# A graph network's last layer: the experts' loop by three chunks instead of four, its ends written out, and the node rows summed tile by tile

## The chip, the cores and the metric

The kernel runs on one core of a Trainium2 chip. The metric is the device time of one execution in microseconds (us), the lower the better. The engines are TensorE (PE, with its weight loads listed apart as PEld), VectorE (DVE), ScalarE (ACT), GpSimd (POOL) and SyncE (SP), which here only issues transfers.

## The reference

Four residual layers over a graph with 3125 nodes of 256 features and 50000 edges, each closed by a layernorm. The change concerns the last layer: a graph convolution, then a mixture of 64 experts, two for each node, then a batch norm over all nodes:

```python
x = gc + (feats @ W_res + b_res)
vals, idx = jax.lax.top_k(x @ Wg + bg, 2)
gates = softmax(vals)
# for each expert e: rows of the nodes that picked it
h1 = gelu(rows @ w1[e] + b1[e])          # 256 -> 512
h2 = h1 @ w2[e] + b2[e]                  # 512 -> 256
core = zeros.at[tok].add(gate * h2)
y = x + core
y = (y - mean(y, 0)) * rsqrt(var(y, 0) + 1e-5) * gamma + beta
```

All weights are float32. The 6250 picked rows fall on the 64 experts very unevenly, from 10 to 409 rows each on the inputs used. Cut into chunks of at most 128 rows of one expert each they make 81 chunks.

## The kernel before

Nodes are held in T = 25 tiles of 128 rows. The last layer ("l3") goes over these tiles: PE adds up the neighbours' rows, DVE makes the tile's rows x (`l3_x4`, L1749, into V; POOL copies them to X4), picks the two experts and gives each row a slot (`l3_top`, `l3_slots`), and POOL scatters the rows to their slots in device memory (`expert_rows_in`). Then the five engines run the functions `sync_moe`, `pe_moe`, `act_moe`, `dve_moe` and `pool_moe`, each in its own order, tied by semaphores.

The experts' loop goes over chunks c. `RING` = 4 is at once the number of chunks written out in one turn of the loop and the number of buffers for a chunk's loads: its rows `xin` (128 KB), `w1s` and `w2s` (512 KB each), the bias `b2s` (128 KB, one row spread over the partitions) and its result `yout`. The transposed rows xTs, the hidden values hTs and their three places in PSUM have two buffers each. The turns are the number of chunks over RING, rounded up.

- PE, for each c: `turn(c+2)` transposes the rows of the chunk two ahead (L554), `hidden(c+1)` makes 512 hidden columns from w1 (L562), `rows_out(c)` multiplies them by w2 (L572). Its queue is in order, so what `turn` waits for (`rows_in`) holds up all that follows.
- ACT: `gelu` (L619). DVE: copies the transposed rows (L659), scales the bias (L683), evicts the result times the gate into yout (L688, which counts `chunk_made` up), and adds yout to the running sum V2 (L694). POOL scatters yout to device memory (L760).
- SP, for each c, in this order, with n = c mod RING:

```python
ex = expert_of(c + RING)
e.wait_ge(S("chunk_turned"), c + 1)
load_rows(c + RING, n)                  # L473
e.wait_ge(S("hidden_summed"), c + 1)
load_w1(ex, n)                          # L476
e.wait_ge(S("chunk_made"), c + 3)       # counted up by 2 beforehand: chunk c is evicted
load_w2(ex, n)                          # L480
load_b2(ex, n)                          # L484
```

SP too is in order: the rows of chunk c+1+RING are issued after the w2 and the bias of chunk c+RING, and so after the eviction of chunk c.

Ahead of the loop DVE copies two chunks' transposed rows, then adds up the node rows X4 over all tiles into R2 (L667, L668), clears V2, and takes the picks and gates that PE has transposed (L582, L671, L672). The loop runs past its end: PE and ACT do a hidden stage for one chunk too many and PE two transposes too many, and SP loads RING chunks that nobody uses. After the loop V2 += R2 (L698), PE sums that over the partitions (L597), DVE subtracts the mean (L703), SP waits for the spare loads (L517) and for the stored rows (L521) and loads the experts' rows back (L526), and DVE, ACT and PE finish the batch norm and the layernorm.

Of the kernel before, what the change touches and what calls it, by code (L numbers as in the profile page):

```python
# [24 lines left out]
P = 128  # L25
# [7 lines left out]
RING = 4  # L33
# [19 lines left out]
def gnn_program(nc, A, out):  # L53
# [33 lines left out]
    NCH = MAXCH + RING  # L87

# [12 lines left out]
    with ExitStack() as ctx:  # L101
# [78 lines left out]
        nturn = sb("nturn", [1, 1], I32)  # L180
# [118 lines left out]
        for base, lot, room in ((mw, ((w1s, (KF, H), RING), (w2s, (HT, F), RING)), T * PARTS * F * 2),  # L299
                                (mx, ((yout, (F,), RING), (b2s, (F,), RING), (xTs, (F,), 2), (hTs, (HT, P), 2),  # L300
                                      (xin, (F,), RING)), 10240)):
# [11 lines left out]
        at = 2 * F * (2 * RING + 2) + 2 * 2 * HT * P  # L313
# [23 lines left out]
        pdec, px4 = psum[:, 5, P:2 * P], psum[:, 5, 0:F]  # L337

# [63 lines left out]
        def past(ph, name):  # L402
            return T * SIGNALS[name].index(ph)
# [63 lines left out]

        def sync_moe(e):
# [53 lines left out]
            e.wait_ge(S("gelu_made"), RING * turns + 1)  # L522
# [18 lines left out]
        def pe_moe(e):  # L541
# [9 lines left out]
            def turn(c, j, n, par):  # L551
                e.wait_ge(S(f"rows_in{n}"), 16 * j + 16)
                for k in range(KF):
                    mm = e.transpose(psum[:, par, k * P:(k + 1) * P], xin[n][:, k * P:(k + 1) * P], identF[:, :])  # L554
                mm.then_inc(S("chunk_turned"), 1)

            def hidden(c, j, n, par):
                e.wait_ge(S("chunk_copied"), c + 1)
                e.wait_ge(S(f"w1_in{n}"), 16 * j + 16)
                for h in range(HT):  # L560
                    for k in range(KF):
                        mm = e.matmul(psum[:, 2 + par, h * P:(h + 1) * P], w1s[n][:, k, h * P:(h + 1) * P],  # L562
                                      xTs[par][:, k * P:(k + 1) * P], start=(k == 0), stop=(k == KF - 1))
                mm.then_inc(S("hidden_summed"), 1)

            def rows_out(c, j, n, par):
                e.wait_ge(S("gelu_made"), c + 1)
                e.wait_ge(S(f"w2_in{n}"), 16 * j + 16)

                e.wait_ge(S("chunk_made"), c + 1)  # L570
                for h in range(HT):
                    mm = e.matmul(psum[:, 4 + par, 0:F], hTs[par][:, h, :], w2s[n][:, h, :],  # L572
                                  start=(h == 0), stop=(h == HT - 1))
                mm.then_inc(S("chunk_summed"), 1)

            turns = e.value_load(nturn[0:1, 0:1], min_val=1, max_val=MAXCH // RING)
# [30 lines left out]
        def act_moe(e):  # L607
# [7 lines left out]
            def gelu(c, par):  # L615
                ex = e.value_load(etab[0:1, bass.ds(c, 1)], min_val=0, max_val=NE - 1)
                e.wait_ge(S("hidden_summed"), c + 1)
                for h in range(HT):
                    mm = e.activation(hTs[par][:, h, :], psum[:, 2 + par, h * P:(h + 1) * P], ACT.Gelu,  # L619
                                      bias=b1T[:, h, bass.ds(ex, 1)])  # L620
                mm.then_inc(S("gelu_made"), 1)

            turns = e.value_load(nturn[0:1, 0:1], min_val=1, max_val=MAXCH // RING)
            gelu(0, 0)
            with e.Fori(0, turns) as j:
                for n in range(RING):
                    c, par = RING * j + n, n % 2

                    e.wait_ge(S("chunk_summed"), c)
                    gelu(c + 1, 1 - par)  # L630
# [14 lines left out]
        def dve_moe(e, st):  # L645
# [3 lines left out]
            st.done(e.tensor_scalar(eint[0:1, 0:1], pages[0:1, 0:1], float(RING - 1), None, ALU.add))  # L649
            st.done(e.tensor_scalar(nturn[0:1, 0:1], eint[0:1, 0:1], RING.bit_length() - 1, None,  # L650
                                    ALU.arith_shift_right))

# [4 lines left out]
            def copy_turned(c, par):  # L657
                e.wait_ge(S("chunk_turned"), c + 1)
                e.tensor_copy(xTs[par], psum[:, par, 0:F]).then_inc(S("chunk_copied"), 1)  # L659

            e.sem_inc(S("chunk_made"), 2)
            copy_turned(0, 0)
            copy_turned(1, 1)


            e.wait_ge(S("tile_x4_kept"), past("l3", "x4_kept") + T)
# [3 lines left out]
            e.wait_ge(S("ids_turned"), 1)  # L670
            e.tensor_copy(pick_of, psum[:, 6, 0:NCH]).then_inc(S("picks_known"), 1)  # L671
            st.done(e.tensor_copy(gate_of, psum[:, 6, NCH:2 * NCH]))  # L672
            turns = e.value_load(nturn[0:1, 0:1], min_val=1, max_val=MAXCH // RING)
            with e.Fori(0, turns) as j:
                for n in range(RING):
                    c, par = RING * j + n, n % 2

                    e.wait_ge(S("hidden_summed"), c + 1)
                    copy_turned(c + 2, par)
# [6 lines left out]
                    e.wait_ge(S(f"rows_stored{n}"), 16 * j)  # L686
                    carry_wait(e)
                    e.scalar_tensor_tensor(yout[n], psum[:, 4 + par, 0:F], gate_of[:, bass.ds(c, 1)], b2s[n], ALU.mult, ALU.add)\  # L688
                        .then_inc(S("chunk_made"), 1)

                    e.wait_ge(S("rows_added"), c + 1)
                    e.wait_ge(S("chunk_made"), c + 3)
# [43 lines left out]
        def pool_moe(e):  # L736
# [11 lines left out]
            turns = e.value_load(nturn[0:1, 0:1], min_val=1, max_val=MAXCH // RING)  # L748
            with e.Fori(0, turns) as j:
                for n in range(RING):  # L750
                    c, par = RING * j + n, n % 2
# [6 lines left out]
                    e.wait_ge(S("chunk_made"), c + 3)  # L758
# [610 lines left out]
        def _(e):  # L1369
# [364 lines left out]

            e.memset(rooms[:, 0, :], float(P))
# [13 lines left out]
            def l3_x4(i, par):  # L1749
# [3 lines left out]
                e.tensor_tensor(V[:, :], pD[0], bc["gc"][:, :], ALU.add).then_inc(S("tile_x4_made"), 1)  # L1753

# [240 lines left out]
```

## Time and profile before

| | us |
|---|---|
| median of 3 runs (1962.0 to 1967.8) | 1963.7 |
| the profiled execution | 1963.03 |
| its span in the trace | 1961.3 |
| PE busy | 1768.7 |
| PEld busy | 1423.0 |
| DVE busy | 949.3 |
| POOL busy | 492.8 |
| ACT busy | 486.4 |

The last layer's tiles end near 1538 us, the experts' loop lies between about 1551 and 1888 us, and the rest, to 1961.3 us, is the batch norm, the layernorm and the stores of the result. In the rows below a line of code is L and its number. An SPq row is a transfer being issued by SP. A PE duration in the timeline overlaps with its neighbours, while the chain's rows lie end to end.

### The profile page before, as it was taken

To read this page: it belongs to the slowest core of one execution; us is meant where nothing else is said; L and a number is where in the kernel's file an instruction comes from. 1 tells how busy PE (TensorE), PEld (TensorE's weight loads), DVE (VectorE), ACT (ScalarE), POOL (GpSimd) and SP (SyncE) were. 2 spreads that over 40 slices of the span, in tenths; PEclk is the share of its full clock that TensorE was granted. 3 is DMA by queue.
4 is the path that set the end of the run, shared out by engine and by line. 5 is a ranking of instruction groups with operands and counts; after the bars stand their busy time and mean duration, and the time that the engine had idled before them with its cause. 6 is when DMAs were issued, how large, how long until landed. Compare 5 with 4: busy or idle time off the path is not lost.

```text
span 1961.3 us, 34807 instructions
## 1 busy us (share of the span) xinstructions
PE 1768.7 (90%) x9576; PEld 1423.0 (73%) x9577; DVE 949.3 (48%) x2841; ACT 486.4 (25%) x1278; POOL 492.8 (25%) x905
## 2 busy tenths in 40 slices
PE   4888887699989999999999999999999599999961
PEld 2455555588878888788888878877777488888851
DVE  7876664444445511121221127766666734434456
ACT  0144444322223311122221111111212132233223
POOL 1122222311113300000000002217778733233314
PEclk7999998799999999999999999999999799999976
DMA  4189999899869888766658878887776499999992
GB/s 133 41 285 307 315 318 344 299 325 325 308 231 374 325 310 288 266 217 217 206 197 304 288 274 290 292 280 237 246 261 214 145 350 377 375 375 375 373 363 69
DMA packets 276800, 545.13 MB, mean 278 GB/s; under 512 B 18358, under 2 KB 201184, under 8 KB 272992
## 3 DMA queue, kind: packets, MB, share of 16 engines
q1 hardware_dynamic: 266720, 525.41, 78.6%
q0 software_dynamic: 8032, 17.63, 2.4%
q10 hardware_dynamic: 1952, 0.95, 0.3%
q8 instruction: 43, 0.70, 0.2%
q14 instruction: 53, 0.43, 0.1%
HBM read 415.12 MB, written 128.81 MB: 277 GB/s over the span
## 4 chain that ended last, share of the span: by engine, by line
PE 73%; DVE 11%; DMA 6%; issue 4%; DVEq 2%; SPq 1%; POOL 1%; ACT 1%; ACTq 0%; POOLq 0%
PE psum L1065 41%; PE psum L562 7%; PE psum L572 7%; PE psum L1162 4%; PE psum L957 4%; PE psum L954 3%; PE psum L976 2%; DMA blk<-counts_src_on_rows 2%; PE psum L1144 1%; PE psum L554 1%; PE psum L1173 1%; SPq L783 1%; DMA expert_weights<-expert_rows_out 1%; DMA counts_src_on_rows<-blk 1%; DMA route<-expert_rows_in 1%
## 5 line engine op out<-in xcount | busy, mean ns | idle before, releaser
L1065 PE MATMUL psum<-xsa,blk 128*128 128x512 f32 x2500 | 638.7, 403 | 11.9 <-DVE xsa L1631 9.7
L1065 PEld LDWEIGHTS psum<-xsa,blk 128*128 128x128 f32 x2500 | 456.8, 189 | 99.2 <-issue 12.6
L1065 PE MATMUL psum<-xsb,blk 128*128 128x512 f32 (+1 forms) x1875 | 407.9, 366 | 8.5 <-DMA blk<-counts_src_on_rows 5.2
L1065 PEld LDWEIGHTS psum<-xsb,blk 128*128 128x128 f32 x1875 | 316.1, 190 | 62.1 <-issue 8.6
L1904 POOL TENSOR_SCALAR ve<-mv 128x1 f32<-128x1 f32 x75 | 16.8, 224 | 763.1 <-DVE mv L1607 763.1
L1492 DVE TENSOR_SCALAR onehots<-counts_scratch 128x348 bf16<-128x348 f16 x464 | 161.6, 374 | 86.1 <-issue 45.8
L954 PE MATMUL psum<-onehots 128*128 128x349 bf16 x464 | 149.3, 322 | 38.7 <-DVE onehots L1497 38.2
L957 PE MATMUL psum<-zrow 128*128 128x512 bf16 x464 | 176.1, 389 | 0.0
L562 PE MATMUL psum<-route,expert_weights 128*128 128x128 f32 x1360 | 171.6, 281 | 4.3 <-DVE route L659 4.2
L562 PEld LDWEIGHTS psum<-route,expert_weights 128*128 128x128 f32 x1360 | 162.0, 195 | 6.1 <-DVE route L659 5.0
L572 PE MATMUL psum<-expert_weights,route 128*128 128x256 f32 x672 | 159.0, 380 | 0.0
L619 ACT ACTIVATE route<-psum,b1T 128x128 f32<-128x128 f32 x340 | 96.9, 368 | 235.0 <-PE psum L562 235.0
L760 POOL DMA_INDIRECT expert_rows_out<-route x84 | 82.7, 984 | 224.7 <-DVE route L688 218.7
L572 PEld LDWEIGHTS psum<-expert_weights,route 128*128 128x128 f32 x672 | 121.3, 191 | 12.9
L688 DVE SCALAR_TENSOR_TENSOR route<-psum,route 128x256 f32<-128x256 f32 x84 | 40.6, 484 | 182.1 <-PE psum L572 181.9
L1600 DVE SCALAR_TENSOR_TENSOR G<-psum,binv,Lo 128x256 f32<-128x256 f32 x50 | 24.1, 483 | 202.7 <-ACT Lo L1311 202.6
L954 PEld LDWEIGHTS psum<-onehots 128*128 128x128 bf16 x464 | 45.6, 98 | 101.9 <-DVE onehots L1492 74.8
L1318 ACT ACTIVATE tT<-psum 128x256 f32<-128x256 f32 x150 | 57.1, 380 | 217.9 <-PE psum L1144 216.2
L976 PE MATMUL psum<-identR,band_rows 128*128 128x130 f32 x625 | 85.6, 289 | 10.3 <-ACT blk L1251 7.3
L976 PEld LDWEIGHTS psum<-identR,band_rows 128*128 128x128 f32 x625 | 78.9, 199 | 15.6 <-ACT blk L1251 7.7
L1311 ACT ACTIVATE Lo<-psum,binv 128x256 f32<-128x256 f32 x50 | 23.7, 474 | 200.6 <-PE psum L1065 200.6
L1879 POOL CAST band_rows<-digits 128x1044 fp32r<-128x1044 uint8 x50 | 56.3, 1151 | 67.7 <-DVE digits L1526 67.6
(316 smaller groups left out, 2109.2 us busy)
## 6 DMA issues: line engine op xcount, KB each, us to landing
blk<-counts_src_on_rows SPq DMA_DIRECT2D x125, 832.0 KB, 5.9
blk<-counts_src_on_rows SPq DMA_DIRECT2D x125, 768.0 KB, 4.8
expert_weights<-in_L_gnn_w SPq DMA_DIRECT2D x176, 512.0 KB, 5.8
blk<-counts_dst_on_rows SPq DMA_DIRECT2D x50, 832.0 KB, 4.4
counts_dst_on_rows<-band_rows SPq DMA_DIRECT2D x25, 1600.0 KB, 8.1
blk<-counts_dst_on_rows SPq DMA_DIRECT2D x50, 768.0 KB, 4.2
counts_src_on_rows<-blk SPq DMA_DIRECT2D x13, 1600.0 KB, 8.7
counts_src_on_rows<-rblk SPq DMA_DIRECT2D x12, 1600.0 KB, 9.7
```

The costliest lines, as they stand in the source:

```text
L562: mm = e.matmul(psum[:, 2 + par, h * P:(h + 1) * P], w1s[n][:, k, h * P:(h + 1) * P], xTs[par][:, k * P:(k + 1) * P], start=(k == 0), stop ...
L572: mm = e.matmul(psum[:, 4 + par, 0:F], hTs[par][:, h, :], w2s[n][:, h, :], start=(h == 0), stop=(h == HT - 1))
L619: mm = e.activation(hTs[par][:, h, :], psum[:, 2 + par, h * P:(h + 1) * P], ACT.Gelu, bias=b1T[:, h, bass.ds(ex, 1)])
L760: e.indirect_dma_start(out=ybuf, out_offset=bass.IndirectOffsetOnAxis(ap=pick_col[n][:, 0:1], axis=0), in_=yout[n], in_offset=None).then_i ...
L954: e.matmul(o, one_d[:, u, :], one_s[:, u, 0:FW + 1], start=False, stop=True, skip_group_check=True).then_inc(S("onehots_used"), 1)
L957: e.matmul(psum[:, par, 0:BANK], zrow[:, 0:P], zrow[:, 0:BANK], start=False, stop=True, skip_group_check=True)
L976: mm = e.matmul(psum[:, s + k // 3, o:o + TURNED], band_rows[par][:, t * P:(t + 1) * P], identR[:, :], start=True, stop=True)
L1065: mm = e.matmul(o, blk[n][:, k * P:(k + 1) * P], XS[:, k, :, 0:Fw], start=(k == 0), stop=(k == T - 1 and not own), skip_group_check=True)
L1162: mm = e.matmul(v, l, r, start=(n_ == 0), stop=(n_ == len(pairs) - 1))
L1318: e.activation(o, pick(a, par), func, **kw).then_inc(S("tile_" + sig), 1)
L1492: e.tensor_scalar(one_s[:, u, 0:FW], iota_f, scol[:, bass.ds(c, 1)], wcol[:, bass.ds(c, 1)], ALU.is_equal, ALU.mult).then_inc(S("sources_r ...
L1879: e.tensor_copy(fields_of(band_rows[par], m), digit(m)).then_inc(S("lower_cast"), 1)
```

## The change

RING is 3. All buffers of the loop, in SBUF and in PSUM, are three (of the three places for transposed rows one shares a bank with a place for results, and one wait is there for it). The number of turns is worked out by a multiplication and a shift, as 3 is no power of two. On PE, ACT and DVE the first or the last turn, or both, are written out beside the loop, without the parts that would run past the end; SP's loop has one turn fewer, so no spare chunks are loaded. The picks' transposes come after the first `rows_out`. The node rows are added to R2 in `l3_x4`, tile by tile, and the loop adds yout to R2 itself; V2, the reduction ahead of the loop and the addition after it are gone. SP's order within a chunk is as it was.

```diff
-RING = 4
+RING = 3
...
+        turned = [psum[:, n, 0:F] for n in (0, 1, 6)]
+        summed = [psum[:, 2 + n, :] for n in range(RING)]
+        made_rows = [psum[:, 2 + RING + n, 0:F] for n in range(RING)]
...
         def sync_moe(e):
...
-            turns = e.value_load(nturn[0:1, 0:1], min_val=1, max_val=MAXCH // RING)
-            with e.Fori(0, turns) as j:
+            turns, ending = turns_of(e), last_turn_of(e)
+            with e.Fori(0, ending) as j:
                 for n in range(RING):
                     c = RING * j + n
                     ex = expert_of(c + RING)
...
                     e.wait_ge(S("hidden_summed"), c + 1)
                     load_w1(ex, n)
 
-                    e.wait_ge(S("chunk_made"), c + 3)
+                    e.wait_ge(S("chunk_made"), c + 1 + RING)
                     load_w2(ex, n)
                     load_b2(ex, n)
...
-                    e.wait_ge(S(f"{name}{n}"), 16 * turns + 16)
+                    e.wait_ge(S(f"{name}{n}"), 16 * turns)
...
         def pe_moe(e):
...
-            turn(0, 0, 0, 0)
-            turn(1, 0, 1, 1)
-            hidden(0, 0, 0, 0)
-            e.wait_ge(S("inputs_loaded"), 16 * (LOADS + 2))
-            for a in range(2):
-                mm = e.transpose(psum[:, 6, a * NCH:(a + 1) * NCH], pick_rows[0:NCH, :, a], identF[0:NCH, 0:NCH])
-            mm.then_inc(S("ids_turned"), 1)
-            with e.Fori(0, turns) as j:
+            turn(0, 0)
+            turn(0, 1)
+            hidden(0, 0, 0)
+
+            def chunks(j, ends=False, starts=False):
                 for n in range(RING):
                     c = RING * j + n
-                    par = n % 2
-
-                    e.wait_ge(S("chunk_copied"), c + 1)
-                    turn(c + 2, j + (n + 2) // RING, (n + 2) % RING, par)
-
-                    e.wait_ge(S("gelu_made"), c)
-                    hidden(c + 1, j + (n + 1) // RING, (n + 1) % RING, 1 - par)
-                    rows_out(c, j, n, par)
-
-            e.wait_ge(S("node_sums"), 1)
-            e.matmul(psum[:, 0, 0:F], ones[:, :], V2[:, :], start=True, stop=True).then_inc(S("bn_summed"), 1)
+                    if not (ends and n + 2 >= RING):
+                        if n == 0 and not starts:
+
+                            e.wait_ge(S("chunk_made"), c + 2)
+                        turn(j + (n + 2) // RING, (n + 2) % RING)
+                    if not (ends and n + 1 >= RING):
+                        hidden(c + 1, j + (n + 1) // RING, (n + 1) % RING)
+                    rows_out(c, j, n)
+                    if n == 0 and starts:
+                        e.wait_ge(S("inputs_loaded"), 16 * (LOADS + 2))
+                        for a in range(2):
+                            mm = e.transpose(pids[a], pick_rows[0:NCH, :, a], identF[0:NCH, 0:NCH])
+                        mm.then_inc(S("ids_turned"), 1)
+            chunks(0, starts=True)
+            with e.Fori(1, ending) as j:
+                chunks(j)
+            chunks(ending, ends=True)
+
+            e.wait_ge(S("rows_added"), RING * turns + T + 1)
+            carry_wait(e)
+            e.matmul(psum[:, 0, 0:F], ones[:, :], R2[:, :], start=True, stop=True).then_inc(S("bn_summed"), 1)
...
         def dve_moe(e, st):
...
-            e.sem_inc(S("chunk_made"), 2)
...
-            st.done(e.tensor_reduce(R2[:, :], X4[:, 0:T - 1, :].rearrange("p t f -> p f t"), AX.X, ALU.add))
-            st.done(e.scalar_tensor_tensor(R2[:, :], X4[:, T - 1, :], valid[:, T - 1:T], R2[:, :], ALU.mult, ALU.add))
-            e.memset(V2[:, :], 0.0).then_inc(S("rows_added"), 1)
...
+                    if not (ends and n + 2 >= RING):
+                        e.wait_ge(S("hidden_summed"), c + 1)
+                        copy_turned(c + 2, (n + 2) % RING)
+                    if n == 0 and starts:
+                        e.wait_ge(S("ids_turned"), 1)
+                        e.tensor_copy(pick_of, pids[0]).then_inc(S("picks_known"), 1)
+                        st.done(e.tensor_copy(gate_of, pids[1]))
+
+                        e.sem_inc(S("chunk_made"), RING)
...
-                    e.tensor_tensor(V2[:, :], V2[:, :], yout[n], ALU.add).then_inc(S("rows_added"), 1)
-
-            e.wait_ge(S("rows_added"), RING * turns + 1)
-            carry_wait(e)
-            e.tensor_tensor(V2[:, :], V2[:, :], R2[:, :], ALU.add).then_inc(S("node_sums"), 1)
+                    e.tensor_tensor(R2[:, :], R2[:, :], yout[n], ALU.add).then_inc(S("rows_added"), 1)
...
                 e.tensor_tensor(V[:, :], pD[0], bc["gc"][:, :], ALU.add).then_inc(S("tile_x4_made"), 1)
+
+                e.wait_ge(S("tile_x4_made"), past("l3", "x4_made") + i + 1)
+                e.wait_ge(S("rows_added"), i + 1)
+                if i < T - 1:
+                    e.tensor_tensor(R2[:, :], R2[:, :], V[:, :], ALU.add).then_inc(S("rows_added"), 1)
+                else:
+                    e.scalar_tensor_tensor(R2[:, :], V[:, :], valid[:, i:i + 1], R2[:, :], ALU.mult, ALU.add)\
+                        .then_inc(S("rows_added"), 1)
```

## Rows read from the trace of the kernel before

**Rows 1.** Busy time of each engine in a stretch of the loop, with its columns.

```profile
core 0: us, PE busy (x) PEld busy (x) DVE busy (x) ACT busy (x) POOL busy (x), PEclk, DMA share, GB/s
1700.00:1750.00 50.00, 50.00 (x341) 44.47 (x340) 19.66 (x52) 14.82 (x52) 15.28 (x26) 1.00 1.08 375
```

**Rows 2.** The chain that ended last, in order of time: start, us, what.

```profile
1603.31 0.22 PE psum L554 x2
1603.53 1.79 PE psum L562 x16
1605.31 1.73 PE psum L572 x8
...
1884.27 1.84 PE psum L562 x16
```

**Rows 3.** Who waited for whom in the loop: total us, times, longest.

```profile
SPq L480 <- DVE route L688: 87.6, 84, 9.7
...
PEld psum L554 <- DMA route<-expert_rows_in: 6.9, 28, 1.5
```

**Rows 4.** Timeline late in the loop: start, us, engine, line, what, idle before.

```profile
1873.31 0.38 SPq L480 DMA_DIRECT2D expert_weights<-in_L_gnn_w  x1
...
1875.43 0.35 SPq L473 DMA_DIRECT2D route<-expert_rows_in  x1
...
1876.26 0.20 PEld L554 LDWEIGHTS psum<-identF,route 128*128 128x128 f32 x2 [0.27 <-issue]
...
1880.41 0.48 DVE L688 SCALAR_TENSOR_TENSOR route<-psum,route 128x256 f32<-128x256 f32 x1 [2.24 <-PE psum L572]
...
1880.92 0.38 SPq L480 DMA_DIRECT2D expert_weights<-in_L_gnn_w  x1
...
1882.72 0.34 SPq L473 DMA_DIRECT2D route<-expert_rows_in  x1
```

**Rows 5.** The rows' loads at L473: durations of issue, and time from issue to landing.

```profile
L473 SPq DMA_DIRECT2D route<-expert_rows_in x88: 340/346/438, 1547.2 to 1886.4; - x88
...
DMA to landing us min/median/max: 2.2/5.0/5.7
```

**Rows 6.** Timeline at the loop's start.

```profile
1551.01 3.04 PE L562 MATMUL psum<-route,expert_weights 128*128 128x128 f32 x16
1551.30 10.82 DVE L667 TENSOR_REDUCE R<-X 128x256 f32<-128x6144 f32 x1
...
1566.95 3.58 PE L562 MATMUL psum<-route,expert_weights 128*128 128x128 f32 x16 [4.24 <-DVE route L659]
...
1567.89 0.38 SPq L480 DMA_DIRECT2D expert_weights<-in_L_gnn_w  x1
...
1572.92 0.38 SPq L480 DMA_DIRECT2D expert_weights<-in_L_gnn_w  x1
```

**Rows 7.** Transfers issued at 1569.77, 1568.69 and 1574.72: the last number is us to landing.

```profile
route<-expert_rows_in SPq DMA_DIRECT2D x1, 128.0 KB, 3.3
expert_rows_out<-route POOLq DMA_INDIRECT x1, 4.0
...
route<-expert_rows_in SPq DMA_DIRECT2D x1, 128.0 KB, 3.7
```

**Rows 8.** Timeline of the last layer's tiles: DVE waiting after `l3_x4`.

```profile
1527.53 0.23 DVE L1761 TENSOR_TENSOR U<-psum,bgb 128x64 f32<-128x64 f32 x1 [1.92 <-PE psum L1162]
```

**Rows 9.** The loop's end: PE's last group in the timeline, and a link of the chain.

```profile
1885.95 1.89 PE L572 MATMUL psum<-expert_weights,route 128*128 128x256 f32 x8
...
1889.28 5.95 DMA expert_rows_out<-route
```

**Rows 10.** Busy time in two early stretches, with the granted clock; columns as in Rows 1.

```profile
100.00:130.00 30.00, 25.21 (x157) 15.23 (x156) 21.48 (x78) 11.60 (x23) 7.12 (x8) 1.00 0.84 285
...
320.00:370.00 50.00, 24.81 (x119) 20.05 (x119) 19.92 (x55) 24.17 (x59) 19.48 (x13) 0.62 0.91 312
```

**Rows 11.** PE's waits in the first of these two stretches: total us, times, longest.

```profile
PE psum L954 <- DVE onehots L1497: 4.8, 3, 1.8
```

More of the change, by code:

```diff
@@ L87, in gnn_program @@
     NCH = MAXCH + RING
+    PART_BITS = 16
+    PART = (1 << PART_BITS) // RING + 1
+    assert all(n * PART >> PART_BITS == n // RING and n * PART < 1 << 24 for n in range(MAXCH + RING))
     YROWS = -(-TOP * NP // (P * (T - 3)))
@@ L299, in gnn_program @@
         for base, lot, room in ((mw, ((w1s, (KF, H), RING), (w2s, (HT, F), RING)), T * PARTS * F * 2),
-                                (mx, ((yout, (F,), RING), (b2s, (F,), RING), (xTs, (F,), 2), (hTs, (HT, P), 2),
+                                (mx, ((yout, (F,), RING), (b2s, (F,), RING), (xTs, (F,), RING), (hTs, (HT, P), RING),
                                       (xin, (F,), RING)), 10240)):
@@ L337, in gnn_program @@
         pdec, px4 = psum[:, 5, P:2 * P], psum[:, 5, 0:F]
+        turned = [psum[:, n, 0:F] for n in (0, 1, 6)]
+        summed = [psum[:, 2 + n, :] for n in range(RING)]
+        made_rows = [psum[:, 2 + RING + n, 0:F] for n in range(RING)]
+        pids = [psum[:, 7, a * NCH:(a + 1) * NCH] for a in range(2)]
+        assert RING == 3 and 2 * NCH <= BANK
         block = ctx.enter_context(nc.Block())
@@ L521, in sync_moe @@
                 e.wait_ge(S(f"rows_stored{n}"), 16 * turns)
-            e.wait_ge(S("gelu_made"), RING * turns + 1)
+            carry_wait(e)
+            e.wait_ge(S("gelu_made"), RING * turns)
             carry_wait(e)
@@ L549, in pe_moe, with turn, hidden @@
             carry_wait(e)
-            def turn(c, j, n, par):
+            def turn(j, n):
                 e.wait_ge(S(f"rows_in{n}"), 16 * j + 16)
                 for k in range(KF):
-                    mm = e.transpose(psum[:, par, k * P:(k + 1) * P], xin[n][:, k * P:(k + 1) * P], identF[:, :])
+                    mm = e.transpose(turned[n][:, k * P:(k + 1) * P], xin[n][:, k * P:(k + 1) * P], identF[:, :])
                 mm.then_inc(S("chunk_turned"), 1)
-            def hidden(c, j, n, par):
+            def hidden(c, j, n):
                 e.wait_ge(S("chunk_copied"), c + 1)
@@ L567, in rows_out @@
                 e.wait_ge(S("gelu_made"), c + 1)
                 e.wait_ge(S(f"w2_in{n}"), 16 * j + 16)
-                e.wait_ge(S("chunk_made"), c + 1)
+                if not isinstance(c, int) or c >= RING - 1:
+                    e.wait_ge(S("chunk_made"), c + 1)
                 for h in range(HT):
-                    mm = e.matmul(psum[:, 4 + par, 0:F], hTs[par][:, h, :], w2s[n][:, h, :],
+                    mm = e.matmul(made_rows[n], hTs[n][:, h, :], w2s[n][:, h, :],
                                   start=(h == 0), stop=(h == HT - 1))
@@ L618, in gelu, with chunks @@
                 for h in range(HT):
-                    mm = e.activation(hTs[par][:, h, :], psum[:, 2 + par, h * P:(h + 1) * P], ACT.Gelu,
+                    mm = e.activation(hTs[n][:, h, :], summed[n][:, h * P:(h + 1) * P], ACT.Gelu,
                                       bias=b1T[:, h, bass.ds(ex, 1)])
                 mm.then_inc(S("gelu_made"), 1)
-            turns = e.value_load(nturn[0:1, 0:1], min_val=1, max_val=MAXCH // RING)
+            turns, ending = turns_of(e), last_turn_of(e)
             gelu(0, 0)
-            with e.Fori(0, turns) as j:
-                for n in range(RING):
-                    c, par = RING * j + n, n % 2
+            def chunks(j, ends):
+                for n in range(RING - 1 if ends else RING):
+                    c = RING * j + n
                     e.wait_ge(S("chunk_summed"), c)
-                    gelu(c + 1, 1 - par)
+                    gelu(c + 1, (n + 1) % RING)
+            with e.Fori(0, ending) as j:
+                chunks(j, False)
+            chunks(ending, True)
             for g, (lo, hi) in enumerate(COMBINED):
@@ L655, in dve_moe, with copy_turned, chunks @@
             e.sem_inc(S("experts_known"), 1)
-            def copy_turned(c, par):
+            def copy_turned(c, n):
                 e.wait_ge(S("chunk_turned"), c + 1)
-                e.tensor_copy(xTs[par], psum[:, par, 0:F]).then_inc(S("chunk_copied"), 1)
-            e.sem_inc(S("chunk_made"), 2)
+                e.tensor_copy(xTs[n], turned[n]).then_inc(S("chunk_copied"), 1)
             copy_turned(0, 0)
             copy_turned(1, 1)
-            e.wait_ge(S("tile_x4_kept"), past("l3", "x4_kept") + T)
-            st.done(e.tensor_reduce(R2[:, :], X4[:, 0:T - 1, :].rearrange("p t f -> p f t"), AX.X, ALU.add))
-            st.done(e.scalar_tensor_tensor(R2[:, :], X4[:, T - 1, :], valid[:, T - 1:T], R2[:, :], ALU.mult, ALU.add))
-            e.memset(V2[:, :], 0.0).then_inc(S("rows_added"), 1)
[L670 to L674, printed above, removed]
-                for n in range(RING):
-                    c, par = RING * j + n, n % 2
-                    e.wait_ge(S("hidden_summed"), c + 1)
-                    copy_turned(c + 2, par)
+            turns, ending = turns_of(e), last_turn_of(e)
+            def chunks(j, ends=False, starts=False):
+                for n in range(RING):
+                    c = RING * j + n
+                    if not (ends and n + 2 >= RING):
[6 more added lines that the diff above has]
+                        e.sem_inc(S("chunk_made"), RING)
                     e.wait_ge(S(f"b2_in{n}"), 16 * j + 16)
@@ L685, in dve_moe @@
                     e.wait_ge(S("chunk_summed"), c + 1)
-                    e.wait_ge(S(f"rows_stored{n}"), 16 * j)
+                    if not starts:
+                        e.wait_ge(S(f"rows_stored{n}"), 16 * j)
                     carry_wait(e)
-                    e.scalar_tensor_tensor(yout[n], psum[:, 4 + par, 0:F], gate_of[:, bass.ds(c, 1)], b2s[n], ALU.mult, ALU.add)\
+                    e.scalar_tensor_tensor(yout[n], made_rows[n], gate_of[:, bass.ds(c, 1)], b2s[n], ALU.mult, ALU.add)\
                         .then_inc(S("chunk_made"), 1)
-                    e.wait_ge(S("rows_added"), c + 1)
-                    e.wait_ge(S("chunk_made"), c + 3)
+                    e.wait_ge(S("rows_added"), c + T + 1)
+                    e.wait_ge(S("chunk_made"), c + 1 + RING)
                     carry_wait(e)
-                    e.tensor_tensor(V2[:, :], V2[:, :], yout[n], ALU.add).then_inc(S("rows_added"), 1)
-            e.wait_ge(S("rows_added"), RING * turns + 1)
-            carry_wait(e)
-            e.tensor_tensor(V2[:, :], V2[:, :], R2[:, :], ALU.add).then_inc(S("node_sums"), 1)
+                    e.tensor_tensor(R2[:, :], R2[:, :], yout[n], ALU.add).then_inc(S("rows_added"), 1)
+            chunks(0, starts=True)
+            with e.Fori(1, ending) as j:
+                chunks(j)
+            chunks(ending, ends=True)
             e.wait_ge(S("bn_summed"), 1)
@@ L747, in pool_moe @@
             e.wait_ge(S("picks_known"), 1)
[L748 removed]
+            turns, ending = turns_of(e), last_turn_of(e)
             with e.Fori(0, turns) as j:
                 for n in range(RING):
[L751 removed]
+                    c = RING * j + n
                     e.wait_ge(S(f"rows_stored{n}"), 16 * j)
@@ L757, in pool_moe @@
                     e.wait_ge(S("pick_taken"), c + 1)
-                    e.wait_ge(S("chunk_made"), c + 3)
+                    e.wait_ge(S("chunk_made"), c + 1 + RING)
                     carry_wait(e)
@@ L1733, in _ @@
             st4 = Steps(e, S("tile_steps"), 4, 14 * T)
+            e.memset(R2[:, :], 0.0).then_inc(S("rows_added"), 1)
             e.memset(rooms[:, 0, :], float(P))
```

24 lines of the change are left out of this document (15 added, 9 removed).

## The prediction, made before the change was run

> **What bounds the kernel now.** I read first the busy times by stretch, because the change touches only the last 450 us. In the middle of the experts' loop PE is busy for all of the 50 us at full clock, and the DMA engines are over 100% busy at 375 GB/s [rows 1]: both look like the bound. The chain tells them apart. One chunk on PE is two transposes, a hidden stage and a row stage, 0.22 + 1.79 + 1.73 = 3.74 us, end to end. Between the hidden stage at 1603.53 and the one at 1884.27 lie 73 chunks, so a chunk really takes 280.74/73 = 3.85 us [rows 2]. PE thus loses 0.11 us a chunk, and the waits say where: at the transposes, for the chunk's rows [rows 3]. A chunk moves 512 + 512 + 128 + 128 KB in and 128 KB out, 1.44 MB; at 375 GB/s that is 3.84 us. So the loop stands at its DMA rate, with PE 3% below it.
>
> Next I followed one load of rows round its circle, as this is where a depth of buffers matters. SP's w2 load waits for DVE's eviction in every chunk (84 waits, 87.6 us) [rows 3], and the rows of the next chunk are issued behind it. The circle, from [rows 4]: PE's transposes start at 1876.26 and the chunk's eviction at 1880.41, 4.2 us; the eviction and the wake-up of SP take 0.5 (to 1880.92); from the w2 issue to the rows' issue it is 1.8 us, and 2.1 where the loop turns (1873.31 to 1875.43), 1.9 on average; then the rows take L to land; and PE starts some 0.1 us later. Sum 6.7 us + L. With four buffers the order after chunk c-1's eviction is w2 of c+3, then the rows of c+4, which PE transposes two chunks ahead, at the head of iteration c+2. That is three iterations after iteration c-1 began, so three chunks must take at least 6.7 us + L. Check: 3 x 3.85 = 11.5, and the median L is 5.0 [rows 5], which makes the fixed part 6.5. I use 6.6. The circle closes, with L long because the queues are full.
>
> **The change, part by part.** *Three buffers.* SP's order is unchanged, so after chunk c-1's eviction come w2 of c+2 and then the rows of c+3, which PE transposes at the head of iteration c+1. That is only two iterations after c-1 began. Two chunks must now take 6.6 + L, so a chunk takes p = (6.6 + L)/2, unless L is under 0.9 (then PE's 3.74 holds, or the DMA rate's 3.84 if L is under 1.1). No row shows an L that short: of 88 loads the fastest took 2.2 us [rows 5].
>
> What L will be with idler queues is the one open size. Bounds: 2.2 (the minimum, rows with little else moving) and 5.0 (the median with full queues). The nearest rows are at the loop's start, where the queues had drained: w2 issued at 1567.89, the next at 1572.92, 5.03 us apart [rows 6], which is about the spacing that I forecast; the rows issued behind them took 3.3 and 3.7 us [rows 7]. They queue behind the same 512 KB of w2, 128 KB of bias and 128 KB of stored rows as in the changed loop. I take 3.5: p = 5.05 us. The DMA engines are then at 3.84/5.05 = 76%, so such an L is consistent with it.
>
> The Trainium skill (DMA: Bandwidth & Descriptors, Anatomy of one DMA) puts a DMA at about 2.0 us fixed plus its bytes over 436 GB/s. For the 896 KB of w2, bias, stored rows and rows as one train that is an estimate of 4.1 us from the w2 issue; the trace's train took 1.9 + 3.3 = 5.2 [rows 6, 7]. By the rule L would be 2.2 and the time 1983.5; by the row it is 3.3 or more, and I go by the row.
>
> The other loads don't bind: w2 is needed three chunks after its issue, w1 nearly so, and the stored rows' buffer comes round after three chunks, some 15 us, against 4.0 for a store in a drained queue [rows 7]. The added wait of PE's transposes for `chunk_made` (c-2) holds up all of PE's queue behind it, but that eviction lies an iteration back: nothing. The third PSUM places and xTs, hTs remove waits that were met already: nothing, as PE's only lasting wait is for rows [rows 3].
>
> *Chunks.* 84 chunks before (four buffers, 21 turns), 81 now (27 turns of three): three fewer, and at the end no spare hidden stage and transposes.
>
> *The loop's start.* The reduction over X4 (10.82 us on DVE and a second step) goes; DVE's copy behind it came late and held PE for 4.24 us, to 1566.95 [rows 6]. In its place 24 additions of 128x256, about 0.43 us each, stand behind `l3_x4`, where DVE then waits 1.92 us for PE's logits in every tile [rows 8]; hidden there, and 25 x 0.45 = 11 us at most if that cover were gone. The memset of R2 is hidden in the same way. PE reaches the end of chunk 1 near 1563 (estimate: hidden(0) from 1551.0, 3.0 at low clock; hidden(1) and the first row stage 3.7; the picks' transposes and their copies about 2; hidden(2) and the second row stage 3.5), 9 us earlier than before. But it gives most back at once. The w2 load of chunk 3 waits for the first eviction, which is near 1561; the rows of chunk 4 follow 1.9 us later and land at about 1566.4, so chunk 2 ends near 1570.
>
> *Sum.* Chunk 78 is the last whose iteration has a transpose to wait for: from chunk 2 it is 76 chunks, 76 x 5.05 = 383.8, so it ends at 1953.8. Then one hidden and two row stages, 1.79 + 2 x 1.73 = 5.25: PE's last row stage ends at 1959.0. Before it ended at 1885.95 + 1.89 = 1887.84 [rows 9]. That is 71.2 us later.
>
> *The end.* The last store took 5.95 us to land [rows 9], beside four spare chunks' loads; without them the shortest seen, 4.0 [rows 7], so 2.0 us less, and the reloads of the experts' rows start that much earlier. V2 += R2 (some 0.4 us) goes, but lies beside this wait. I count -2.0.
>
> Total: +69.2 us. On the profiled execution's 1963.03, which is 1.7 more than its span, 2032.2; the median of the runs shown lies 0.7 above it, so 2033. In general the time is 1900 + 38 L.
>
> **The rivals.**
>
> *A. The rows land in time* (the other side). If L or the fixed part were shorter than I read, say because PE's transposes don't really wait for the rows that SP has just issued, a chunk would take the DMA rate's 3.84 us. Chunk 78 would end at 1563 + 77 x 3.84 = 1858.7, the last row stage at 1863.9, 23.9 earlier, and with the end's 2.0 the time is 1938. The Trainium skill's list of best practices asks only for double buffers so that DMA and compute overlap; by that rule three suffice and this rival holds. It decides for faster once L is under 1.5 us (1900 + 38 L below 1958). Against it: none of 88 loads of rows landed in under 2.2 us, and the circle reproduces the loop of before to 0.2 us in 11.5. Chance 0.05.
>
> *B. The clock falls.* PE would be idle 1.3 us in each 5.05, busy 74%. A hidden stage that ran after a wait of 4.24 us took 3.58 instead of 1.79 [rows 6]; at the lower of the two levels throughout, a chunk is near 7.5 us and the time 1649 + 76 x 7.5 = 2219. For it: a stretch with PE 50% busy had a mean granted clock of 0.62 of full speed. Against: one with 84% busy kept 1.00 [rows 10], with single waits of up to 1.8 us in it [rows 11]. 74% lies nearer to that. If only a part of the chunks were hit, 2090 to 2219. Chance 0.08.
>
> *C. No change to speak of:* slower chunks just paid for by the start, the end and the three chunks saved. That needs p = 4.14, L = 1.7, again below any row seen. Chance 0.02.
>
> **How the numbers follow.** The forecast, a loop bound by the rows' circle with L between 2.2 and 5.0, has 0.85: 1984 to 2090, likeliest 2033. The range 1985 to 2085 covers it but for its rims and leaves out A, C and nearly all of B. A difference of 0.3%, 6 us, is about what a measurement of this kernel can tell from no change. Faster by more 0.05 (A), within it 0.02 (C), slower 0.93 (the forecast and B).
>
> **What would show it.** Right: a chunk takes about 5 us; PE's wait at its transposes, put down to the rows' load, is the largest of PE, some 1.3 us for each of 78 chunks, about 100 us in total instead of 6.9; the rows' landing median falls from 5.0 to 3.3 to 3.7; the loop moves about 285 GB/s instead of 375; SP still waits for the eviction. The reduction is gone from the loop's start and nothing has grown in the tiles before it. Wrong: PE waits for something else (an eviction, w1 or w2), rows that land in 2.2 us or in 5 (38 us of time for each us), a granted clock below 1.00 in the loop, or a first turn that starts much later than I estimated because code written out has to be fetched.

## The result, and the profile of the changed kernel

The changed kernel takes 2056.32 us (median of 4 runs, 2054.84 to 2064.72) against 1964.68 us (median of 4, 1962.0 to 1967.8) for the kernel before: a ratio of 1.0475, 95% interval [1.0442, 1.0507]. The profiled execution took 2054.84 us, with a span of 2053.1. The forecast was 2033, its range 1985 to 2085.

The same stretch of the loop as in [rows 1], in the changed kernel, with its columns:

```profile
core 0: us, PE busy (x) PEld busy (x) DVE busy (x) ACT busy (x) POOL busy (x), PEclk, DMA share, GB/s
1700.00:1750.00 50.00, 38.52 (x254) 33.04 (x252) 14.70 (x38) 11.44 (x40) 10.63 (x18) 1.00 0.88 279
```

PE is no longer busy throughout and the DMA engines move 279 GB/s instead of 375: neither is the bound now. The waits over the loop and the end name what is (engine, line, waited for: us in total, times, longest), to be read against [rows 3]:

```profile
PEld psum L571 <- DMA route<-expert_rows_in: 135.0, 73, 7.5
PE psum L571 <- DMA route<-expert_rows_in: 105.9, 72, 7.1
...
SPq L496 <- DVE route L717: 186.0, 77, 7.2
```

PE waits at the transposes (now L571) for the rows in nearly every chunk, 105.9 us in all. SP still waits for the eviction (now L717) ahead of w2 (L496). The chain of work shows the circle itself, two chunks long (start, us, what):

```profile
1704.44 0.44 PE psum L571 x2
1704.88 1.79 PE psum L579 x16
1706.67 1.74 PE psum L591 x8
...
1708.53 0.49 DVE route L717
...
1709.04 0.38 SPq L496
...
1709.62 0.36 SPq L500
...
1710.73 0.39 SPq L489
...
1711.13 3.40 DMA route<-expert_rows_in
...
1714.58 0.44 PE psum L571 x2
...
1721.32 3.70 DMA route<-expert_rows_in
```

Read it as a round: transposes, hidden stage and row stage on PE, the eviction, SP's w2 and bias, then the rows (L489), their landing, and the next transposes on the chain 10.14 us later. What lies between two landings is 6.69 us here (1704.44 to 1711.13) and 6.74 in the next round. Of the chain's 38 landings the fastest took 2.9, the median 3.8, the mean 3.9 and the slowest 6.0 us.

At the loop's end PE and SP stand as follows (timeline: start, us, engine, line, what), against [rows 9]:

```profile
1975.52 1.89 PE L591 MATMUL psum<-expert_weights,route 128*128 128x256 f32 x8
...
1979.03 3.62 PE L591 MATMUL psum<-expert_weights,route 128*128 128x256 f32 x16
...
1987.60 2.30 SPq L543 DMA_DIRECT2D expert_weights<-expert_rows_out  x5
```

The chain's link for the last store, which SP's reload at 1987.60 waits for:

```profile
1984.43 2.86 DMA expert_rows_out<-route
```

So the span divides like this. Chunk 2 ends at 1572.85; 76 chunks later chunk 78 ends at 1975.52 + 1.89 = 1977.41, 404.56/76 = 5.32 us each; the last row stage ends at 1979.03 + 3.62 = 1982.65, 5.24 later; from there to the end it is 70.45 us, where it was 1961.3 - 1887.84 = 73.46 before.

### The profile page after: what moved, and what is told of

Same layout as the page of the kernel before. It is cut to its first block, busy times and chain, and to the rows that moved or that the text cites. A ratio compares the mean times of both kernels' runs of the same rounds, so it can differ in the third digit from the quotient of the medians.

```text
span 2053.1 us, 34763 instructions
## 1 busy us (share of the span) xinstructions
PE 1760.6 (86%) x9478; PEld 1412.8 (69%) x9479; DVE 948.9 (46%) x2850; ACT 482.3 (23%) x1262; POOL 495.3 (24%) x899
## 4 chain that ended last, share of the span: by engine, by line
PE 59%; DMA 13%; POOL 9%; issue 6%; DVE 5%; SPq 4%; DVEq 2%; ACT 1%; ACTq 0%; POOLq 0%
PE psum L1095 37%; DMA route<-expert_rows_in 7%; PE psum L579 4%; PE psum L591 4%; PE psum L987 3%; PE psum L1192 3%; DMA blk<-counts_src_on_rows 3%; PE psum L984 3%; POOL expert_rows_in L1965 2%; POOL pick_and_gate_of_row L1982 2%; PE psum L1006 2%; SPq L813 1%; PE psum L1203 1%; DVE route L717 1%; PE psum L571 1%
## 5 line engine op out<-in xcount | busy, mean ns | idle before, releaser
L645 ACT ACTIVATE route<-psum,b1T 128x128 f32<-128x128 f32 x324 | 92.5, 369 | 336.1 <-PE psum L579 336.1
L579 PE MATMUL psum<-route,expert_weights 128*128 128x128 f32 x1296 | 167.0, 285 | 0.1
L591 PE MATMUL psum<-expert_weights,route 128*128 128x256 f32 x648 | 154.7, 382 | 0.3 <-ACT route L645 0.3
L717 DVE SCALAR_TENSOR_TENSOR route<-psum,route 128x256 f32<-128x256 f32 x81 | 39.2, 484 | 225.3 <-PE psum L591 224.9
L571 PE MATMUL psum<-identF,route 128*128 128x128 f32 x162 | 36.3, 308 | 108.0 <-DMA route<-expert_rows_in 105.9
L571 PEld LDWEIGHTS psum<-identF,route 128*128 128x128 f32 x162 | 17.4, 145 | 137.8 <-DMA route<-expert_rows_in 135.0
```

The source lines that it names most:

```text
L571: mm = e.transpose(turned[n][:, k * P:(k + 1) * P], xin[n][:, k * P:(k + 1) * P], identF[:, :])
L579: mm = e.matmul(summed[n][:, h * P:(h + 1) * P], w1s[n][:, k, h * P:(h + 1) * P], xTs[n][:, k * P:(k + 1) * P], start=(k == 0), stop=(k == ...
L591: mm = e.matmul(made_rows[n], hTs[n][:, h, :], w2s[n][:, h, :], start=(h == 0), stop=(h == HT - 1))
L645: mm = e.activation(hTs[n][:, h, :], summed[n][:, h * P:(h + 1) * P], ACT.Gelu, bias=b1T[:, h, bass.ds(ex, 1)])
L717: e.scalar_tensor_tensor(yout[n], made_rows[n], gate_of[:, bass.ds(c, 1)], b2s[n], ALU.mult, ALU.add)\
```

## The experiments

Beside these runs the kernel before took 1966.73, 1966.67 and 1965.58 us (medians of 19, 10 and 11 runs). Ratios are to it.

**The suspected order alone, with four buffers.** The kernel before; only the rows are issued one chunk later, three ahead.

```diff
                     e.wait_ge(S("chunk_turned"), c + 1)
-                    load_rows(c + RING, n)
+                    load_rows(c + RING - 1, (n + RING - 1) % RING)
```

> The kernel before, four buffers of everything and nothing else of the change, but with SP issuing each chunk's rows one chunk later, so three ahead. Theory: the circle spans two iterations, a chunk takes (6.6 + 3.9)/2 = 5.25 us or a little more, and the time is about 1964 + 80 x 1.4 = 2076 us (2060 to 2100), with PE's waits at its transposes above 90 us. Rivals (three weight buffers, code written out, PSUM places make the loss): stays near 1964, at most 1975.

Measured 2091.18 us, ratio 1.063 [1.0597, 1.0662]. The waits of its loop:

```profile
PE psum L554 <- DMA route<-expert_rows_in: 107.3, 73, 3.1
```

One line of the kernel before gives the changed kernel's wait, with all four buffers there. So the order alone makes a loss of this size, without three buffers, code written out or third PSUM places. The time is 15 us above the expected 2076. The landing isn't the reason: the expectation counts 3.9, and 29 landings on its chain between 1575 and 1880 us had a median of 3.9. In the profiled execution (2096.15 us) the clock accounts for most of it: in stretches with a granted clock of 0.92 to 0.97 eight hidden stages on the chain took 2.6 to 3.4 us instead of 1.79, which with the row stages behind them makes some 14 us.

**The additions alone, tile by tile.** The kernel before with only the node rows' sum moved into the tiles.

```diff
-            st.done(e.tensor_reduce(R2[:, :], X4[:, 0:T - 1, :].rearrange("p t f -> p f t"), AX.X, ALU.add))
...
+                    e.tensor_tensor(R2[:, :], R2[:, :], V[:, :], ALU.add).then_inc(S("node_rows"), 1)
```

> The kernel before with one part of the change alone: the node rows are added up tile by tile in the last layer and the reduction ahead of the experts' loop is gone. Theory: PE's wait of 4.24 us at the loop's start and the half-clock stage behind it go, 5 to 9 us, time 1955 to 1960. Rival: the DMA rate of the loop sets its end, so the earlier start is lost again within some chunks: 1962 to 1965. Second rival: the 25 additions are not hidden in the tiles and cost up to 11 us: 1965 to 1972.

Measured 1960.01 us, ratio 0.9974 [0.996, 0.9989]: a small gain, at the upper end of the theory's range. The interval reaches into the first rival's range (a part of the earlier start lost again) and excludes the second. The additions cost the tiles nothing: from the first `l3_x4` to the last it is 214.9 us with them in this run, and 217.5 without them in the kernel before and in the run above. Why the tiles got shorter, 0.1 us each, is not shown.

**Rows one chunk earlier, three buffers.** The changed kernel; SP issues each chunk's rows one chunk earlier, ahead of the wait for an eviction that they stood behind.

```diff
+            e.wait_ge(S("chunk_turned"), 1)
+            load_rows(RING, 0)
...
-                    e.wait_ge(S("chunk_turned"), c + 1)
-                    load_rows(c + RING, n)
+                    e.wait_ge(S("chunk_turned"), c + 2)
+                    load_rows(c + 1 + RING, (n + 1) % RING)
```

> The changed kernel, with SP issuing the rows' load one chunk further ahead (the rows of chunk c+4 where it issued those of c+3; still three buffers of everything). Theory (the rows' circle): the circle spans three iterations again, so the loop falls back to its DMA rate of 3.84 us a chunk; with 81 chunks and the shorter start the time is about 1940 us (1930 to 1955), and PE's wait at its transposes falls from 106 us to under 15. Rival 1 (three buffers are too few for the weights): w1 or w2 then lands late instead, the time stays above 2020. Rival 2 (what costs is the written-out code or the third PSUM places): no change from 2056.

Measured 1975.16 us, ratio 1.0051 [1.0028, 1.0075]. 81 of the 92 us come back, but it is a miss: the theory gave 1930 to 1955, and its first rival, late weights, above 2020. Its waits and one stretch of its loop (columns as above) say what is late next:

```profile
PE psum L581 <- DMA expert_weights<-in_L_gnn_w: 23.1, 33, 1.2
...
PEld psum L573 <- DMA route<-expert_rows_in: 5.7, 10, 1.0
```

```profile
1700.00:1750.00 50.00, 46.61 (x314) 41.83 (x313) 18.15 (x48) 13.68 (x48) 13.28 (x24) 1.00 1.00 340
```

The hidden stage (L581) now waits for w1, which is still issued behind the eviction of the chunk before.

**Rows ahead of the bias.** The changed kernel with the rows between w2 and the bias, 1.5 us earlier in SP's order but still behind the eviction.

```diff
                     load_w2(ex, n)
+                    e.wait_ge(S("chunk_turned"), c + 2)
+                    load_rows(c + 1 + RING, (n + 1) % RING)
                     load_b2(ex, n)
```

> The changed kernel, with the rows' load issued between the w2 and the bias load after the same eviction, instead of behind both and the next chunk's table read. The circle still spans two iterations but is shorter by 1.3 us of issue and by the bias's 0.35 us of transfer. Theory: a chunk takes half of that less, 5.32 - 0.85 = 4.5 us, and the time is about 1992 us (1980 to 2005), between the changed kernel and the first experiment. Rivals (weights late, code, PSUM places): no change from 2056.

Measured 2030.52 us, ratio 1.033 [1.030, 1.036]: a miss. The issue did move (timeline):

```profile
1704.05 0.38 SPq L496 DMA_DIRECT2D expert_weights<-in_L_gnn_w  x1
...
1704.64 0.34 SPq L489 DMA_DIRECT2D route<-expert_rows_in  x1
...
1709.36 0.44 PE L572 MATMUL psum<-identF,route 128*128 128x128 f32 x2 [0.42 <-DMA route<-expert_rows_in]
```

But the rows, issued 0.59 us after w2 instead of some 2, took a median of 4.8 us to land on the chain (30 landings) instead of 3.8. Of the 1.5 us by which the issue moved, 1.0 was lost again in the landing.

**Half of w2.** What is in that landing time? The changed kernel with 256 KB less issued ahead of the rows.

```diff
-                    load_w2(ex, n)
+                    load_half_w2(ex, n)     # w2s[n][:, 0:HT // 2, :] only
```

> The changed kernel, with only the first 256 KB of w2 loaded for each chunk in the loop (the second half stays that of the first chunks, so the output is another). It asks what the time from issue to landing of the rows, 3.9 us, consists of. Theory (the rows queue behind the bytes that SyncE issued just before them): 256 KB fewer at 375 GB/s are 0.7 us, so the rows land 0.7 us sooner, a chunk takes 0.35 us less, 4.95 instead of 5.3, and the time falls by some 26 us, to 2030 (2020 to 2040). Rival (it is a latency of their own, whatever stands ahead of them): the landing stays near 3.9 us and the time above 2048.

Measured 2022.84 us, ratio 1.0294 [1.0263, 1.0326]. 29 landings on its chain (1575 to 1880 us) had a mean of 3.27 us; the same stretch of the changed kernel had 29 with a mean of 3.88. So 256 KB fewer ahead take 0.6 us off the landing, near the 0.7 expected: that part is not a latency of the rows' own. What the other 3.3 us consist of is not shown. The landing alone gives 0.3 us a chunk, 23 us of the 33 by which the time fell; up to 5 us of the rest are the clock, at 1.00 from 1600 to 1880 us here, and not throughout in the changed kernel (next section).

**Rows issued by ScalarE.** The changed kernel; SP keeps the weights and the bias.

```diff
             def chunks(j, ends):                 # ScalarE
                 for n in range(RING - 1 if ends else RING):
                     c = RING * j + n
+                    if not ends:
+                        e.wait_ge(S("chunk_turned"), c + 2)
+                        load_rows(c + 1 + RING, (n + 1) % RING)
```

> The changed kernel; the rows' loads are issued by ScalarE (one chunk earlier, between two activations) in place of SyncE; SyncE keeps w1, w2 and the bias. Theory (the rows were late since they stood in SyncE's order behind w2 and the bias, which wait for the eviction): the rows come in time, as they did with the issue one chunk earlier on SyncE (1975 us), and w1, with one issue fewer ahead of it, a little earlier than there: 4.1 to 4.3 us a chunk, 1955 to 1980 us. Rival 1 (three buffers are too few for any order): at or above 2030 us. Rival 2 (ScalarE's issue delays the activations, which TensorE's last matmuls wait for): 1985 to 2020 us, with TensorE's wait at L591 for ScalarE.

Measured 1975.98 us, ratio 1.0047 [1.003, 1.0064], the time of the earlier issue on SP, and with the same wait left:

```profile
PE psum L577 <- DMA expert_weights<-in_L_gnn_w: 25.6, 30, 2.7
```

What counts is which waits stand ahead of the issue, not whose queue it is. The Trainium skill (DMA: Bandwidth & Descriptors, Issuing engines are not separate DMA queues) says that issuing from several engines saves only the time of the issue itself. The two runs agree with it: the same order from one engine took 1975.16 us, from two 1975.98. The 80 us gained over the changed kernel come from the wait for the eviction, which no longer stands ahead of the issue, on either queue.

**Rows and w1 one chunk earlier.** The first fix, with w1 moved along:

```diff
+                    ahead, ex = expert_of(c + 1 + RING), expert_of(c + RING)
...
-                    e.wait_ge(S("hidden_summed"), c + 1)
-                    load_w1(ex, n)
+                    e.wait_ge(S("hidden_summed"), c + 2)
+                    load_w1(ahead, (n + 1) % RING)
```

> The changed kernel with its three buffers; SyncE issues the rows and w1 of a chunk one chunk earlier, ahead of the wait for the eviction, so that only w2 and the bias still stand behind it. Theory (what costs the time is how far ahead the loads are issued, not the count of buffers): with rows alone moved, the wait had gone to w1 (336 GB/s, 4.27 us a chunk); now both circles span three iterations, nothing is late any more, and the loop stands at the DMA rate of before (1.44 MB at 375 GB/s, 3.84 us a chunk): about 1943 us, 1935 to 1950, faster than both kernels, DMA 365 to 375 GB/s between 1600 and 1850. Rival (three buffers are too few, wherever the loads are issued, since w2 and the store come next): at or above 1965 us, with TensorE's wait gone to the rows' matmul L591 for w2.

Measured 1949.45 us, ratio 0.9909 [0.9879, 0.9938]: faster than both kernels, by 0.9% than the one before, with three buffers. The stretch again, back at the rate of [rows 1] (between 1600 and 1700 us it is 348 and then 363 GB/s, under the 365 to 375 expected):

```profile
1700.00:1750.00 50.00, 49.81 (x339) 44.12 (x338) 19.92 (x52) 14.72 (x53) 15.34 (x26) 1.00 1.07 373
```

**Without GpSimd's additions.** The changed kernel without `X += beta` (L776) ahead of the loop, to explain a late first eviction (last section).

> The changed kernel without GpSimd's five additions of beta to X ahead of the loop (the beta is left out of the output). Theory (the first bias scale L711 took 3.56 us, until GpSimd's last addition ended, since the two engines stood in each other's way): L711 takes 0.34 us like the later ones, the first eviction comes some 3 us earlier, and TensorE's wait of 7.1 us for the rows of chunk 3 or 4 shrinks to about 4; the time falls by some 3 us, to about 2053. Rival (L711 was late for something else): L711 still takes over 3 us and nothing moves.

Measured 2049.73 us (one run), some 3 us below the 2053 expected. The first eviction came 10.4 us after the first transposes instead of 14.3, and PE's wait shrank from 7.1 us to 2.4. DVE's first bias scale in the changed kernel, and in this one:

```profile
1556.03 3.56 DVE L711 TENSOR_SCALAR route<-route 128x256 f32<-128x256 f32 x1 [0.26 <-DVE route L705]
```

```profile
1556.56 0.35 DVE L711 TENSOR_SCALAR route<-route 128x256 f32<-128x256 f32 x1 [0.26 <-DVE route L705]
...
1557.10 0.48 DVE L717 SCALAR_TENSOR_TENSOR route<-psum,route 128x256 f32<-128x256 f32 x1 [0.19 <-DVE route L711]
```

**Both together.** Rows and w1 earlier, and the additions cut into tiles between GpSimd's stores:

```diff
+                    if shifts and n < 2:
+                        shift(2 * j + n, 1)      # X[:, tile, :] += beta, first twelve turns
```

> Three buffers with the rows and w1 issued one chunk earlier (1949 us, 0.9909 of before), and GpSimd's additions of beta to X cut into tiles of 128x256 and put between its stores, two in each of the first twelve turns of the loop. Theory (the first eviction was late since the additions held up DVE's bias scale, and a late first eviction costs the loop's start): the first eviction comes 3 to 4 us earlier, counted from the first transposes, as without the additions, and the loop, at its DMA rate, doesn't feel the additions of some 0.6 us each: 1942 to 1947 us, 0.3% less than without this. Rival 1 (the additions now delay stores or evictions throughout the early loop): 1949 to 1955 us. Rival 2 (at the DMA rate the queues make up for a late first eviction): 1949 us, no difference.

Measured 1945.08 us, ratio 0.9893 [0.9872, 0.9913], the lowest median. The first eviction came 10.8 us after the first transposes, without the spread 14.4. From the first transposes to the end of the last row stage its profile has 322.2 us, without the spread 327.0; the intervals of the two ratios overlap, so the runs alone don't tell this step from nothing.

## Why the prediction came out as it did

*The mechanism* held. Against the forecast in the profile's time, a span of 2030.5, the end came 22.6 us later. The terms:

- *Chunk time, forecast 5.05, measured 5.32*: 76 x 0.27 = 20.7 us, nearly all of it, in three parts. Between the chain's landings that begin at 1711.13 and 1910.67 the granted clock was 1.00 and a chunk took 5.25 us, with a mean L of 3.77 and a fixed part of 2 x 5.25 - 3.77 = 6.73. So L, taken as 3.5 from two drained loads at the loop's start [rows 7], was 0.27 too small, 10 us over 76 chunks; the fixed part, taken as 6.6, was 0.13 too small, 5 us. Landings in this stretch lay between 2.9 and 4.4, and the 3.3 and 3.7 of [rows 7] are two of such a scatter. The last 5.5 us lie in the other 38 chunks and are the clock: there four hidden stages on the chain took 2.9 to 3.3 us instead of 1.79, mostly at the lower of the granted clock's two levels (1.2 and 2.4 GHz), which with the row stages behind them makes 6 us. One of them, with the transposes ahead of it, and the granted clock of two stretches (columns as above):

```profile
1687.32 0.57 PE psum L571 x2
1687.89 3.29 PE psum L579 x16
```

```profile
1600.00:1650.00 50.00, 38.26 (x240) 32.94 (x238) 14.62 (x37) 11.08 (x40) 10.79 (x18) 0.97 0.83 268
1650.00:1700.00 50.00, 37.93 (x242) 33.24 (x243) 15.41 (x40) 10.29 (x36) 11.92 (x20) 0.97 0.82 267
```

  PE had waited 1.9 to 2.4 us for rows just before each of the four; stages behind other waits as long ran at full speed.
- *The estimate by the Trainium skill* (DMA: Bandwidth & Descriptors, Anatomy of one DMA), an L of 2.2: no landing on the chain was that short, the fastest took 2.9. That section gives its fit for transfers that GpSimd issues, and these are SP's.
- *Start*: chunk 2 ended at 1572.85, forecast near 1570. The loop began early: the first transposes started at 1545.47, at 1549.81 before. Of that, 2.7 us lie ahead of the last layer's tiles (first `l3_x4` at 1313.80 instead of 1316.46), where executions of the same code scatter: among the profiled kernels with three buffers that share all code up to the loop, the first transposes lie anywhere from 1545.20 to 1550.66. Another 2.9 us are the shorter tiles, and from the last `l3_x4` to the first transposes it took 1.2 us longer. Against the early start, the first eviction came only at 1559.78, 14.3 us after the first transposes, as L711 was held up (last section), and PE then stood idle until the rows behind that eviction landed, at 1566.57, where the forecast had 1566.4. So the early start and the late eviction cancelled by chance. Nearly all of the difference at the end of chunk 2 arose behind that idle time: the transposes, the hidden and the row stage took 0.69, 3.41 and 2.17 us on the chain, where the forecast counted 0.22, 1.79 and 1.73 (timeline, the last brackets: idle before, and for what; then the chain):

```profile
1559.78 0.48 DVE L717 SCALAR_TENSOR_TENSOR route<-psum,route 128x256 f32<-128x256 f32 x1 [0.19 <-DVE route L711]
...
1562.15 0.34 SPq L489 DMA_DIRECT2D route<-expert_rows_in  x1
...
1566.57 0.69 PE L571 MATMUL psum<-identF,route 128*128 128x128 f32 x2 [7.12 <-DMA route<-expert_rows_in]
```

```profile
1567.26 3.41 PE psum L579 x16
1570.67 2.17 PE psum L591 x8
```

- *Last stages*: 5.24, forecast 5.25. *End*: -3.0, forecast -2.0; the last store landed in 2.86 us, below the 4.0 that I took for its minimum. *Additions*: no cost, as forecast, and shown by the run with them alone; that the tiles would get shorter was not forecast.
- *Of the signs named ahead*: PE's wait 105.9 us (about 100), DMA rate 279 GB/s in the stretch shown and 273 from 1600 to 1850 us (285), SP waiting for the eviction, now 186.0 us. The rows' landing was a little above the 3.3 to 3.7 named.

*Rival A, rows in time*, was wrong of this kernel, and the experiments give its price: with rows and w1 in time three buffers take 1949.45, where A had worked out 1938. So the bare count of buffers was not the cause; the count together with SP's order was. With rows alone in time, w1 binds. The prediction says that w2 is needed three chunks after its issue and w1 "nearly so". In the changed kernel w1 is issued at 1711.41 for a hidden stage that starts at 1720.10, 8.7 us or 1.6 chunks later; w2 has 2.5 chunks. That was enough there, where the rows are later, so that w1 didn't bind; with the rows put right it does, at 4.24 us a chunk (1.44 MB at 340 GB/s) instead of 3.84. *Rival B, the clock*: it came, but small. A few stages ran at the lower level, 5.5 us over the chunks and about 2 at the start, where B had priced a partial fall at 57 us and more. *Rival C* needed 4.14 us a chunk, and 5.32 were measured.

## What to carry to other kernels

Count how many iterations each load's circle spans, from the event that allows its issue, through everything ahead of it in the issuing queue, to its use; taking one buffer away shortens that span by one, and a loop that stood at its DMA rate can become bound by a latency while both DMA and TensorE go idle. Before buying buffers back, issue first the loads whose buffers are free already, ahead of the wait for a later event: here that gave three buffers a better time than the kernel before with four. That the gain comes from the buffers is not shown: by an estimate the three chunks saved (3 x 3.84 = 11.5 us) and the additions (6.7 us by themselves) are enough for the 17 us gained, and four buffers with the earlier issue were not run. When the first load is in time, work out the next circle before expecting the whole gain.

## What the runs showed of the hardware

A DVE instruction from SBUF to SBUF was held up by GpSimd's work, longer than by the one instruction that was running. GpSimd's last two additions and an earlier copy on DVE, in the timeline of the changed kernel:

```profile
1546.19 0.85 DVE L690 COPY route<-psum 128x256 f32<-128x256 f32 x2 [2.30 <-PE psum L571]
...
1553.70 2.89 POOL L776 TENSOR_TENSOR X<-X,bc_bet 128x1280 f32<-128x1280 f32 x1
...
1556.56 2.88 POOL L776 TENSOR_TENSOR X<-X,bc_bet 128x1280 f32<-128x1280 f32 x1
```

L711 began at 1556.03, during GpSimd's fourth addition of 2.89 us; the fifth, begun at 1556.56, ran ahead of it, and L711 ended at 1559.59, just after that one. It takes 0.345 us as a rule (median of 81). Without the additions it took 0.35, and from the first transposes to the end of chunk 2 it was 21.69 us instead of 27.38. DVE's copies out of PSUM went at their usual speed beside the same additions (two in 0.85 us above; one takes 0.42). The Trainium skill (SBUF — State Buffer, SBUF: two separate sides) describes a port pair that DVE and GpSimd hold in turn, whole instructions at a time. By that rule L711 should wait for one addition. The trace agrees on the blocking, and shows a second addition, right behind the first, going ahead of the waiting instruction. With rows and w1 earlier the same instruction took 3.70 us, again to just after the fifth addition; with the additions spread, one of its later instances began beside a single addition of 0.74 us and took 0.90. That the port pair is the reason is the skill's account; the runs show only that the additions are.
